# 59 tiles of 512 rows and 11 of 256 in the expert part, in place of 67 of 512

## The chip, the core and the metric

One core of a Trainium2 chip runs the whole kernel in one launch. The metric is the device time of that launch in microseconds. TensorE (PE), VectorE (DVE), ScalarE (ACT), GpSimd (POOL) and SyncE (SP) each run their own list of instructions in order and meet at semaphores. SP starts the loads; POOL starts the scattered stores. The order of all lists is written out by hand.

## What is computed

128 sequences of 124 tokens (15,872 tokens, 256 features) go through a tokenizer, one attention layer and a mixture of six experts of which each token uses two:

```
h = _L0_tok_ref(x, W, b, gamma, beta)
h = h + _L0_attn_ref(_layernorm(h), ...)          # 124 x 124 scores per sequence
# _L0_ffn_ref(f = _layernorm(h)), E = 6, TOP_K = 2:
rh = relu(f @ router_w1 + router_b1)
expert_logits = softmax(rh @ router_w2 + router_b2)
top_w, top_i = top_k(expert_logits, 2);  routing_weights = softmax(top_w)
h1 = relu(f @ expert_w1[e] + expert_b1[e])
h2 = relu(h1 @ expert_w2[e] + expert_b2[e])
expert_out = h2 @ expert_w3[e] + expert_b3[e]
h = h + sum over the two chosen experts of routing_weight * expert_out
```

So 31,744 pairs of token and expert go through three 256 x 256 layers. Every product is made three times, with high and low halves of both factors (hi*hi, hi*lo, lo*hi), to reach float32 accuracy on the fast path of TensorE.

## The kernel before

The **first part** (`pipeline(step)`) works through the sequences in 32 groups of four. Each token's normed features, its gates and its number are written by POOL (line 522) into `expert_rows`, a DRAM tensor with one region per expert, so that the rows of an expert stand together. `h` itself is stored to `out`.

The **second part** runs over `NT` = 67 tiles of `TILE` = 512 rows: the most that six experts can need when each one's last tile is filled up with pad rows. The first six tiles (`EARLY`) belong to the expert that leads after group 19 and start inside the first part. For the rest DVE makes a table on the chip (`tile_table_rows`, `tile_table_experts`: the row at which tile t starts, its expert, whether weights and biases change, and `ADD_AT`, the count of landed stores to wait for), SP writes it to DRAM and reads it back into `tab`.

Four steps make up one tile t:

- *turn* (line 782): TensorE transposes 4 x 2 blocks of `xg` into banks 0 and 1; ACT copies them to `xv` and makes `x_hi` (986, 989), DVE makes `x_lo` (1380).
- *first layer* (793), 12 products of 512 columns (2 output halves x 2 input halves x 3 variants) into banks 2 and 3; ACT makes `h1v` (996), DVE splits it into `h1_hi` and `h1_lo` (1395, 1380).
- *second layer* (793), 12 such products into banks 4 and 5; ACT makes `h2v` (1003), DVE splits it.
- *third layer* (820), 24 products of 256 columns into banks 6 and 7; DVE adds the bias into `yo` (1411), ACT multiplies by the gate (1009), POOL adds the 4 x 128 rows to `out` with four indirect stores that accumulate (570).

TensorE's order in step t is: first layer of t, turn of t+1, third layer of t-1, second layer of t. DVE's is: split h1 of t, low half of x of t+1 (`rows_low`), sums of t-1 (`rows_out`), split h2 of t. ACT's is: `h1v` of t, `xv` and `x_hi` of t+1, `h2v` of t, gates of t-1. Below, F, T, Th and S are short for first layer, turn, third layer and second layer.

POOL's `add_tile(t)` waits until the stores of tile t-2 have landed, because two experts' tiles may hold the same token. If tile t begins a new expert, it waits also for the stores of t-1 (`ADD_AT`). Tiles of one expert never share a token, so there the stores run on. `yo` has four buffers, `tail` (gates and token numbers) eight, `xg` and `small` four, `w_sb` two. SP loads 512 rows (530 KB) for each tile and 3 x 512 KB of weights only where the expert differs from that of two tiles before (`cond=`).

Of the kernel before, what the change touches and what calls it, by code (L numbers as in the profile page):

```python
# [11 lines left out]

# [16 lines left out]
P = 128  # L29
# [4 lines left out]
D = 256  # L34
# [14 lines left out]
TB = TILE // P  # L49
REGION = NTOK + TILE  # L50
NT = (NTOK * TOPK + NE * (TILE - 1)) // TILE
# [13 lines left out]
SPARE = NT - NTOK * TOPK // TILE  # L65
# [4 lines left out]
NORMS = 3  # L70
DRAIN = G + 1
assert (DECIDE + 1) * GT * TOPK > NE * (EARLY * TILE - 1)
# [16 lines left out]
def audio_tower(nc, x, tok_w, tok_b, tok_gamma, tok_beta, wq, bq, wk, bk, wv, bv, scale,  # L89
                rw1, rb1, rw2, rb2, eweights, esmall, out):  # L90
    with ExitStack() as ctx:  # L91
# [10 lines left out]
        tab_dram = nc.dram_tensor("tile_table", [NT, COLS], I32, kind="Internal").ap()  # L102

# [65 lines left out]
        tail = sb("tail", [P, TAILS, TB, REC - D])  # L169

# [6 lines left out]
        with ExitStack() as part_a:  # L177
# [37 lines left out]
            "tail_kept", "y_ps", "y_dve", "y_gated", "dve_passed", "pool_passed", "sp_passed")}  # L215
# [61 lines left out]
        def landed(t):  # L277

            return (t // 2 + 1) * ADDED if t >= 0 else 0

# [7 lines left out]
        def _(sp):  # L288
# [134 lines left out]
            def next_rows(t):  # L423
                if t < NT:
                    wait_apart(sp, S["txT_ps"], (t - SLOTS + 1) * 2, S["sp_passed"])
                    wait_apart(sp, S["tail_kept"], (t - SLOTS + 1) * 2, S["sp_passed"])
                    if t < EARLY:
                        early_rows(t)
                    else:
                        load_rows(t % SLOTS, table_of(t, ROW, NE * REGION + (SPARE - 1) * TILE))  # L430

# [7 lines left out]
            for t in range(SLOTS, EARLY):  # L439
                wait_apart(sp, S["y_dve"], (t - SLOTS + 1) * 4, S["sp_passed"])  # L440
# [10 lines left out]

            for t in range(1, NT):
                if EARLY <= t + WSLOTS < NT:
                    wait_apart(sp, S["h1_ps"], (t + 1) * 2, S["sp_passed"])
                    load_layers(t + WSLOTS, (0,))
                if t + SLOTS + 1 > EARLY:
                    next_rows(t + SLOTS + 1)
                if EARLY <= t + 1 < NT:
                    wait_apart(sp, S["y_ps"], t * 2, S["sp_passed"])
                    load_layers(t + 1, (2,))  # L460
                if EARLY <= t + SLOTS - 1 < NT:
                    wait_apart(sp, S["y_dve"], t * 4, S["sp_passed"])
                    load_small(t + SLOTS - 1)
                if EARLY <= t + WSLOTS < NT:
                    wait_apart(sp, S["h2_ps"], (t + 1) * 2, S["sp_passed"])
                    load_layers(t + WSLOTS, (1,))
            for i in range(2):
                sp.wait_ge(y_added[i], (NT - i + 1) // 2 * ADDED)

        @block.gpsimd  # L470
        def _(pool):
# [86 lines left out]
            def add_tile(t):  # L558

                wait(pool, y_added[t % 2], landed(t - 2))  # L560
                if t < EARLY:
                    wait(pool, y_added[(t - 1) % 2], landed(t - 3))
                else:
                    if t == EARLY:
# [904 lines left out]
```

## Time and profile before

| | us |
|---|---|
| median of three runs | 1250.46 (1249.2 to 1252.42) |
| the profiled execution | 1249.82 |
| span in its trace | 1248.0 |
| TensorE busy | 1197.6 (96%) |
| VectorE / ScalarE / GpSimd busy | 984.9 / 893.4 / 901.1 |

TensorE's granted clock was 0.989 of full speed over the span. The page says what each engine does in the whole; the stretch views cut the span into parts; the timeline gives single instructions with start, duration and, in brackets, the idle time before them and what ended it; the view of waits sums that idle time.

### The profile page before, as it was taken

What the parts mean: (1) busy time and instruction counts of PE and PEld (TensorE: products, weight loads), DVE (VectorE), ACT (ScalarE), POOL (GpSimd) and SP (SyncE); (2) the same over time, 40 slices, a digit from 0 to 9 for tenths busy, and PEclk for the clock granted to TensorE, in tenths of its full rate; (3) what the DMA queues carried; (4) which work ended last, traced back from release to release, by engine and by line L of the source; (5) the groups of instructions that cost most, each with busy time, mean ns of one, the idle gap of its engine ahead of it and who ended that gap; (6) DMA issues with size and microseconds to landing.
All of it is one profiled execution on the core that took longest, in us unless ns stands there. A gap on an engine that the chain in (4) does not pass through costs nothing. (4 is left out here: it accounts for less than half of the span.)

```text
span 1248.0 us, 27869 instructions
## 1 busy us (share of the span) xinstructions
PE 1197.6 (96%) x7792; PEld 1060.7 (85%) x7792; DVE 984.9 (79%) x3213; ACT 893.4 (72%) x2093; POOL 901.1 (72%) x684
## 2 busy tenths in 40 slices
PE   6999999999999999999789999999999999999993
PEld 5888988889888988887678888889888888888883
DVE  5678888888888988886796887778778777787773
ACT  4788888888888888887456667666676666766762
POOL 2227888888888888887788676767667667676776
PEclk9999999999999999999899999999999999999997
DMA  4334665554454545564589988776886797697655
GB/s 132 111 94 121 164 166 148 143 128 131 128 128 123 129 130 142 169 168 117 139 189 279 238 155 206 119 128 108 174 180 113 130 225 126 116 203 150 111 60 60
DMA packets 137190, 180.43 MB, mean 145 GB/s; under 512 B 38344, under 2 KB 103500, under 8 KB 137036
## 3 DMA queue, kind: packets, MB, share of 16 engines
q0 software_dynamic: 75456, 69.19, 34.5%
q1 hardware_dynamic: 60316, 108.67, 28.6%
q8 instruction: 63, 1.03, 0.3%
q10 hardware_dynamic: 1264, 0.79, 0.2%
q14 instruction: 91, 0.75, 0.2%
HBM read 159.01 MB, written 101.49 MB: 209 GB/s over the span
## 5 line engine op out<-in xcount | busy, mean ns | idle before, releaser
L570 POOL DMA_INDIRECT out<-yo,tail x268 | 432.5, 1614 | 169.1 <-issue 139.6
L522 POOL DMA_INDIRECT expert_rows<-rec,row_i x256 | 356.3, 1392 | 78.0 <-issue 67.2
L1003 ACT ACTIVATE h2v<-bank,small 128x512 f32<-128x512 f32 x134 | 92.3, 690 | 205.3 <-PE bank L793 189.8
L820 PE MATMUL bank<-w_sb,h_hi 128*128 128x256 f32 x1072 | 208.7, 288 | 3.5 <-issue 3.4
L793 PE MATMUL bank<-x_hi,w_sb 128*128 128x512 f32 x536 | 178.2, 394 | 6.1 <-DVE x_lo L1380 4.6
L793 PE MATMUL bank<-h_hi,w_sb 128*128 128x512 f32 x536 | 177.2, 391 | 1.8 <-issue 1.8
L820 PEld LDWEIGHTS bank<-w_sb,h_hi 128*128 128x128 f32 x1072 | 171.3, 191 | 4.4 <-issue 4.3
L820 PE MATMUL bank<-w_sb,h_lo 128*128 128x256 f32 x536 | 151.5, 283 | 0.0
L793 PEld LDWEIGHTS bank<-x_hi,w_sb 128*128 128x128 f32 x536 | 101.7, 190 | 27.9 <-issue 4.8
L793 PEld LDWEIGHTS bank<-h_hi,w_sb 128*128 128x128 f32 x536 | 100.9, 188 | 21.9 <-issue 1.9
L1009 ACT ACTIVATE yo<-yo,gcol 128x256 f32<-128x256 f32 x268 | 113.9, 498 | 4.5 <-DVE yo L1411 4.5
L1395 DVE CAST h_hi<-h1v 128x512 fp32r<-128x512 f32 x134 | 63.8, 476 | 64.1 <-ACT h1v L996 64.0
L584 PE MATMUL bank<-tok_proj,xT_hi 128*124 128x256 f32 x512 | 101.8, 292 | 9.0 <-DVE tok_proj L1029 9.0
L793 PE MATMUL bank<-x_lo,w_sb 128*128 128x512 f32 x268 | 105.2, 393 | 0.0
L793 PE MATMUL bank<-h_lo,w_sb 128*128 128x512 f32 x268 | 105.1, 392 | 0.0
L820 PEld LDWEIGHTS bank<-w_sb,h_lo 128*128 128x128 f32 x536 | 102.7, 192 | 0.0
L1395 DVE CAST h_hi<-h2v 128x512 fp32r<-128x512 f32 x134 | 59.0, 440 | 49.0 <-ACT h2v L1003 43.8
L1380 DVE TENSOR_TENSOR h_lo<-h1v,h_hi 128x512 fp32r<-128x512 f32 x134 | 93.0, 694 | 4.6
L1380 DVE TENSOR_TENSOR h_lo<-h2v,h_hi 128x512 fp32r<-128x512 f32 x134 | 92.9, 694 | 4.6
L584 PE MATMUL bank<-v_proj,xn1T_hi 128*124 128x256 f32 x512 | 94.7, 286 | 0.0
L513 POOL TENSOR_TENSOR rstd<-vareps,neghalf 124x8 f32<-124x8 f32 (+1 forms) x67 | 89.8, 1341 | 5.6
L1063 DVE BATCH_NORM_STATS2 stats<-h 124x6 f32<-124x256 f32 x256 | 89.4, 411 | 0.0
(193 smaller groups left out, 2975.9 us busy)
## 6 DMA issues: line engine op xcount, KB each, us to landing
w_sb<-split_weights SPq DMA_DIRECT2D x189, 512.0 KB
xg<-expert_rows SPq DMA_DIRECT2D x67, 530.0 KB
out<-h SPq DMA_DIRECT2D x32, 496.0 KB
split_weights<-half_w SPq DMA_DIRECT2D x36, 256.0 KB
small<-in_esmall SPq DMA_DIRECT2D x67, 134.0 KB
x_in<-in_x SPq DMA_DIRECT2D x32, 250.0 KB
expert_rows<-pad_rows SPq DMA_DIRECT2D x9, 530.0 KB
raw_w<-in_eweights SPq DMA_DIRECT2D x36, 128.0 KB
```

The source lines that it names most:

```text
L513: pool.tensor_tensor(rstd[0:TOK, norms, :], vareps[0:TOK, norms, :], neghalf[0:TOK, :].unsqueeze(1).to_broadcast([TOK, count, GB]), ALU.po ...
L522: pool.indirect_dma_start(rows_dram, bass.IndirectOffsetOnAxis(ap=row_i[0:TOK, slot, j, k:k + 1], axis=0), rec[0:TOK, slot, j, :], None).t ...
L570: pool.indirect_dma_start(out, bass.IndirectOffsetOnAxis(ap=tail[:, t % TAILS, j, E8:].bitcast(I32), axis=0), yo[:, t % YO, j, :], None, c ...
L584: mm = pe.matmul(bank, lhs[a], rhs[b], start=(first and n == 0), stop=(last and n == 2))
L793: mm = pe.matmul(banks[bank + m][:], w[:, n, c, wh, m * P:(m + 1) * P], act[:, c, :], start=(c == 0 and p == 0), stop=(c == DC - 1 and p = ...
L820: mm = pe.matmul(banks[6 + b][:, (j % 2) * D:(j % 2 + 1) * D], act[:, c, j * P:(j + 1) * P], w[:, 2, c, wh, :], start=(c == 0 and p == 0), ...
L1003: act.activation(h2v[:, m, :], banks[bank + m][:], ACT.Relu, bias=small[:, t % SLOTS, DC + m:DC + m + 1]).then_inc(S["h2_v"], 1)
L1009: act.activation(yo[:, t % YO, j, :], yo[:, t % YO, j, :], ACT.Identity, scale=gcol[:, t % YO, j:j + 1]).then_inc(S["y_gated"], 1)
L1063: v.bn_stats(stats[R, which, j, :], src(j)).then_inc(s, 1)
L1380: v.tensor_tensor(lo, val, hi.bitcast(F32), ALU.subtract).then_inc(ready, 1)
L1395: v.tensor_copy(hi[:, m, :], val[:, m, :]).then_inc(s, 1)
```

## The change

- `NT` becomes 59 tiles of 512 rows, the number that is full of real rows whatever the routing. What is left goes into `NH` = 11 tiles of `HALF` = 256 rows. Together 33,024 rows in place of 34,304.
- `ORDER` is the list of all 70 pieces. A half tile stands behind the big tiles 14, 18, ... 54. Each list of instructions now goes through `ORDER`, with the piece's place `q` in the counts of semaphores and 256 columns where 512 were.
- Half tiles have their own buffers: `half_xg` (one), `half_sb` for weights (one), `half_small` (one), `half_yo` and `half_tail` (two each). SP loads rows, biases and all three weights for each of them, without a condition (`half_rows`, `half_layers`, called from `half_loads` two and one big tiles ahead).
- DVE makes a second table behind piece 4 (`half_table`, 29 small instructions): row, expert, and the store counts `HOLD`, `HOLD_ODD`, `FOLLOW`. It takes a way through DRAM of its own.
- POOL's `add_half` waits for the stores of the big tile ahead of it if that has another expert (`HOLD`); the big tile behind it waits for the half tile's stores if it has another expert (`FOLLOW`).

```diff
-NT = (NTOK * TOPK + NE * (TILE - 1)) // TILE
+NT = (-(-NTOK * TOPK // HALF) - NE) // 2
+NH = (NTOK * TOPK + NE * (HALF - 1)) // HALF - 2 * NT
...
+FIRST_HALF, HALF_STEP = 14, 4
+HALF_RING = 2
...
+AFTER = [FIRST_HALF + HALF_STEP * k for k in range(NH)]
+ORDER = []
+for big in range(NT):
+    ORDER.append(Piece(len(ORDER), False, big, TB))
+    if big in AFTER:
+        ORDER.append(Piece(len(ORDER), True, AFTER.index(big), HB))
...
+            def half_layers(k, layers):
+
+                expert = half_table_of(k, HEXPERT, NE - 1)
+                for n in layers:
+                    if k:
+                        q = HALVES[k - 1].q
+                        wait_apart(sp, (S["h1_ps"], S["h2_ps"], S["y_ps"])[n], (q + 1) * 2, S["sp_passed"])
+                    sp.dma_start(half_sb[:, n, :, :, :].rearrange("p c b n -> p c (b n)").bitcast(F32),
+                                 split_dram[bass.ds(expert * (3 * DC) + n * DC, DC), :, :].rearrange("q p n -> p q n")
+                                 ).then_inc(half_w_loaded[n], 16)
+            def half_loads(t):
...
+                for k in range(NH):
+                    since = t - (FIRST_HALF + HALF_STEP * (k - 1))
+                    if since == 2:
+                        half_rows(k)
+                        half_layers(k, (0,))
+                    if since == 3:
+                        half_layers(k, (1, 2))
...
             def add_tile(t):
...
+                if t.n - 1 == AFTER[0] or t.n - 2 in AFTER:
+                    pool.wait_ge(S["half_added"], sum(a < t.n for a in AFTER) * HALF_ADDED)
+                elif t.n - 1 in AFTER:
+                    at = half_value(AFTER.index(t.n - 1), FOLLOW)
+                    wait_apart(pool, S["half_added"], at, S["pool_passed"])
+                add_rows(t, y_added[t.n % 2])
+            def add_half(t):
+
+                if t.n == 0:
+                    pool.wait_ge(S["half_tab_loaded"], 16)
+                even, odd = half_value(t.n, HOLD), half_value(t.n, HOLD_ODD)
+                wait_apart(pool, y_added[0], even, S["pool_passed"])
+                wait_apart(pool, y_added[1], odd, S["pool_passed"])
+                add_rows(t, S["half_added"])
...
             def layer(t, n, bank, hi, lo, read, count, done):
-                w = w_sb[t % WSLOTS]
+                w, cols = weights_in(t), t.blocks * P
...
-                            mm = pe.matmul(banks[bank + m][:], w[:, n, c, wh, m * P:(m + 1) * P], act[:, c, :],
+                            mm = pe.matmul(banks[bank + m][:, 0:cols], w[:, n, c, wh, m * P:(m + 1) * P], act[:, c, 0:cols],
                                            start=(c == 0 and p == 0), stop=(c == DC - 1 and p == 2))
```

What stands in a row on TensorE. Before, between the first layer of a tile (lines with `x_hi`, `x_lo`) and its second, there is a turn and a whole third layer (24 products, of which the first stand here):

```order
L793 MATMUL bank<-x_hi,w_sb 128x512
L782 MATMUL bank<-ident,xg 128x128 x8
L820 MATMUL bank<-w_sb,h_hi 128x256
L820 MATMUL bank<-w_sb,h_lo 128x256
L820 MATMUL bank<-w_sb,h_hi 128x256 x2
L820 MATMUL bank<-w_sb,h_lo 128x256
L820 MATMUL bank<-w_sb,h_hi 128x256 x2
L820 MATMUL bank<-w_sb,h_lo 128x256
```

In the changed kernel, at the big tile behind a half tile (`half_sb` holds the half tile's weights):

```order
L961 MATMUL bank<-x_hi,w_sb 128x512
L950 MATMUL bank<-ident,xg 128x128 x8
L989 MATMUL bank<-half_sb,h_hi 128x256
L989 MATMUL bank<-half_sb,h_lo 128x256
L989 MATMUL bank<-half_sb,h_hi 128x256 x2
L989 MATMUL bank<-half_sb,h_lo 128x256
L989 MATMUL bank<-half_sb,h_hi 128x256 x2
L989 MATMUL bank<-half_sb,h_lo 128x256
L989 MATMUL bank<-half_sb,h_hi 128x256 x2
L989 MATMUL bank<-half_sb,h_lo 128x256
L989 MATMUL bank<-half_sb,h_hi 128x256
L961 MATMUL bank<-h_hi,w_sb 128x512
```

The third layer between the two is now 12 products, so the second layer of that big tile stands 12 products nearer to its first.

On POOL, the stores of two tiles in a row before, with the semaphores that each waits for:

```order
L566 TENSOR_LOAD tab [waits y_added0]
L566 ISA x2
L570 DMA out<-yo,tail 16896x256 [waits y_added1,y_gated]
L570 DMA out<-yo,tail 16896x256 x3
L566 TENSOR_LOAD tab [waits y_added1]
L566 ISA x2
L570 DMA out<-yo,tail 16896x256 [waits y_added0,y_gated]
```

And in the changed kernel from a half tile to the big tile behind it:

```order
L735 DMA out<-half_yo,half_tail 16896x256 [waits y_added0,y_added1,y_gated]
L735 DMA out<-half_yo,half_tail 16896x256
L710 TENSOR_LOAD tab [waits y_added1]
L710 ISA x2
L720 TENSOR_LOAD half_tab [waits y_added0]
L720 ISA x2
L735 DMA out<-yo,tail 16896x256 [waits half_added,y_gated]
L735 DMA out<-yo,tail 16896x256 x3
```

Two stores more stand between the tiles' stores, with a wait for both counts of big stores ahead of them and a wait for `half_added` behind them.

On DVE, behind the last split of piece 4's h2, the split of piece 5's h1 came next before:

```order
L1380 TENSOR_TENSOR h_lo<-h2v,h_hi 128x512 [waits h2_split]
L1395 CAST h_hi<-h1v 128x512 [waits h1_v]
L1380 TENSOR_TENSOR h_lo<-h1v,h_hi 128x512 [waits h1_split]
L1395 CAST h_hi<-h1v 128x512 [waits h1_v]
L1380 TENSOR_TENSOR h_lo<-h1v,h_hi 128x512 [waits h1_split]
```

Now the second table stands between them; its first and its last rows are

```order
L1616 TENSOR_TENSOR h_lo<-h2v,h_hi 128x512 [waits h2_split]
L1554 TENSOR_TENSOR u_pairs<-t_nt,t_cum 124x8
L1555 TENSOR_SCALAR u_halves<-t_i 124x8
L1556 TENSOR_SCALAR u_at<-t_iota 124x1
L1558 TENSOR_SCALAR u_next<-t_iota 124x1 x2
L1562 TENSOR_SCALAR u_pairs<-u_pairs 124x8 [waits halves,near]
...
L1610 TENSOR_SCALAR u_cols<-u_cols 124x1 [waits halves]
L1613 CAST u_coli<-u_cols 124x5 [waits halves]
L1633 CAST h_hi<-h1v 128x512 [waits h1_v]
```

The split of piece 5's h1 moved behind 29 small instructions.

## Rows read from the trace of the kernel before

**Rows 1.** Page, part 1: busy us, share of the span, instructions.
```profile
PE 1197.6 (96%) x7792; PEld 1060.7 (85%) x7792; DVE 984.9 (79%) x3213; ACT 893.4 (72%) x2093; POOL 901.1 (72%) x684
```

**Rows 2.** Stretches: length, then busy (count) of PE, PEld, DVE, ACT, POOL; clock, DMA.
```profile
510.00:700.00 190.00, 175.00 (x1106) 151.34 (x1105) 150.40 (x535) 124.27 (x283) 148.52 (x113) 0.98 0.71 181
700.00:1200.00 500.00, 499.90 (x3034) 444.87 (x3033) 396.97 (x867) 332.55 (x652) 356.72 (x221) 1.00 0.77 150
```

**Rows 3.** View of waits, TensorE, 720 to 1240 us: total, times, longest.
```profile
PE bank L820 <- issue: 2.0, 1, 2.0
```

**Rows 4.** Timeline of TensorE over one tile: start, us, instruction.
```profile
901.01 0.40 PE L793 MATMUL bank<-h_hi,w_sb 128*128 128x512 f32 x1
...
903.76 0.39 PE L793 MATMUL bank<-x_hi,w_sb 128*128 128x512 f32 x1
...
906.49 1.03 PE L782 MATMUL bank<-ident,xg 128*128 128x128 f32 x8
907.28 0.36 PE L820 MATMUL bank<-w_sb,h_hi 128*128 128x256 f32 x1
...
907.60 0.40 PE L820 MATMUL bank<-w_sb,h_hi 128*128 128x256 f32 x2
...
907.96 0.40 PE L820 MATMUL bank<-w_sb,h_hi 128*128 128x256 f32 x2
...
910.24 0.40 PE L793 MATMUL bank<-h_hi,w_sb 128*128 128x512 f32 x1
```

**Rows 5.** Timeline of ScalarE and of VectorE over the same tile.
```profile
904.55 1.70 ACT L1009 ACTIVATE yo<-yo,gcol 128x256 f32<-128x256 f32 x4
906.15 1.25 ACT L996 ACTIVATE h1v<-bank,small 128x512 f32<-128x512 f32 x2
...
906.85 0.43 DVE L1395 CAST h_hi<-h1v 128x512 fp32r<-128x512 f32 x1 [1.01 <-ACT h1v L996]
...
908.47 0.69 DVE L1380 TENSOR_TENSOR h_lo<-h1v,h_hi 128x512 fp32r<-128x512 f32 x1
```

**Rows 6.** Timeline near the end: last h2 split, and the third layer behind it.
```profile
1226.85 0.69 DVE L1380 TENSOR_TENSOR h_lo<-h2v,h_hi 128x512 fp32r<-128x512 f32 x1
...
1227.64 0.36 PE L820 MATMUL bank<-w_sb,h_hi 128*128 128x256 f32 x1 [2.01 <-issue]
```

**Rows 7.** Timeline of POOL: stores at new experts (tiles 15, 44, 64) and at 59.
```profile
772.23 1.56 POOL L570 DMA_INDIRECT out<-yo,tail  x1 [5.28 <-issue]
...
1033.24 1.68 POOL L570 DMA_INDIRECT out<-yo,tail  x1 [0.30 <-issue]
1037.97 1.54 POOL L570 DMA_INDIRECT out<-yo,tail  x1 [3.05 <-DMA out<-yo,tail]
...
1174.32 1.66 POOL L570 DMA_INDIRECT out<-yo,tail  x1 [1.83 <-issue]
...
1221.44 1.69 POOL L570 DMA_INDIRECT out<-yo,tail  x1 [2.88 <-DMA out<-yo,tail]
```

**Rows 8.** Stretches as in rows 2, around loads of weights, last two: DMA share, GB/s.
```profile
735.00:767.00 32.00, 32.00 (x190) 28.25 (x189) 26.25 (x57) 20.38 (x40) 25.06 (x16) 1.00 1.01 233
...
1034.00:1038.00 4.00, 4.00 (x30) 3.68 (x29) 2.88 (x6) 4.00 (x10) 0.95 (x2) 1.00 0.58 76
...
660.00:665.00 5.00, 3.55 (x17) 2.58 (x15) 2.52 (x5) 2.97 (x6) 4.39 (x3) 1.00 1.13 317
```

**Rows 9.** Timelines of VectorE (table, first and last) and TensorE around piece 5.
```profile
643.16 0.15 DVE L1362 TENSOR_TENSOR t_cols<-t_row,t_first 124x1 f32<-124x1 f32 x1
...
644.35 0.17 DVE L1377 CAST t_coli<-t_cols 124x5 int32<-124x5 f32 x1
...
655.10 1.09 PE L782 MATMUL bank<-ident,xg 128*128 128x128 f32 x8 [2.27 <-DMA xg<-expert_rows]
...
663.27 0.50 PE L793 MATMUL bank<-x_hi,w_sb 128*128 128x512 f32 x1 [1.45 <-DMA w_sb<-split_weights]
```

**Rows 10.** Page, part 6: issues of weight loads and their size.
```profile
w_sb<-split_weights SPq DMA_DIRECT2D x189, 512.0 KB
```

More of the change, by code:

```diff
@@ L13 @@
+from collections import namedtuple
 from contextlib import ExitStack
@@ L70 @@
 NORMS = 3
+HROW, HEXPERT, HOLD, HOLD_ODD, FOLLOW, HCOLS = range(6)
+HALVES_AT = 27
+FIRST_HALF, HALF_STEP = 14, 4
+HALF_RING = 2
 DRAIN = G + 1
+Piece = namedtuple("Piece", "q half n blocks")
+AFTER = [FIRST_HALF + HALF_STEP * k for k in range(NH)]
+assert AFTER[-1] + 2 < NT and FIRST_HALF % 2 == 0 and HALF_STEP % 2 == 0
+ORDER = []
[3 more added lines that the diff above has]
+        ORDER.append(Piece(len(ORDER), True, AFTER.index(big), HB))
+BIG = [t for t in ORDER if not t.half]
+HALVES = [t for t in ORDER if t.half]
 assert (DECIDE + 1) * GT * TOPK > NE * (EARLY * TILE - 1)
@@ L279, in landed, with gated_up_to, rows_in, kept_tail @@
             return (t // 2 + 1) * ADDED if t >= 0 else 0
+        def gated_up_to(q):
+            return sum(t.blocks for t in ORDER[:max(q, 0)])
+        def rows_in(t):
+            return half_xg[:] if t.half else xg[:, t.n % SLOTS, :, :]
+        def kept_tail(t):
+            return half_tail[:, t.n % HALF_RING, :, :] if t.half else tail[:, t.n % TAILS, :, :]
+        def small_in(t):
+            return half_small[:] if t.half else small[:, t.n % SLOTS, :]
+        def sums_out(t):
+            return half_yo[:, t.n % HALF_RING, :, :] if t.half else yo[:, t.n % YO, :, :]
+        def gate_out(t):
+            return half_gcol[:] if t.half else gcol[:, t.n % YO, :]
+        def weights_in(t):
+            return half_sb if t.half else w_sb[t.n % WSLOTS]
+        def rows_here(eng, t):
+            if t.half:
+                eng.wait_ge(S["half_rows_loaded"], 16 * (t.n + 1))
+            else:
+                eng.wait_ge(rows_loaded[t.n % SLOTS], t.n // SLOTS * 16 + 16)
+        def small_here(eng, t):
+            if t.half:
+                eng.wait_ge(S["half_small_loaded"], 16 * (t.n + 1))
+            else:
+                eng.wait_ge(small_loaded[t.n % SLOTS], t.n // SLOTS * 16 + 16)
+        def layer_here(eng, t, n):
+            if t.half:
+                eng.wait_ge(half_w_loaded[n], 16 * (t.n + 1))
+            else:
+                eng.wait_ge(w_loaded[t.n % WSLOTS][n], fetched(t.n))
+        def added_before(eng, t, ring):
+            if t.half:
+                wait(eng, S["half_added"], (t.n + 1 - HALF_RING) * HALF_ADDED)
+            else:
+                wait(eng, y_added[t.n % 2], landed(t.n - ring))
         def sent_to(slot, groups):
@@ L577, in _ @@
+            for t in ORDER:
+                if t.half:
+                    add_half(t)
+                else:
+                    add_tile(t)
         @block.tensor
@@ L1399, in rows_out @@
             def rows_out(t):
-                at = t * 4
-                wait(v, S["y_gated"], (t - 1) * TB)
-                wait(v, y_added[t % 2], landed(t - YO))
-                v.wait_ge(small_loaded[t % SLOTS], t // SLOTS * 16 + 16)
-                v.tensor_tensor(gsel[:], tail[:, t % TAILS, :, 0:E8],
-                                small[:, t % SLOTS, 2 * DC + D:SMALL].unsqueeze(1).to_broadcast([P, TB, E8]),
+                at, each = t.q * 4, t.blocks // 2
+                gates_of = half_gsel[:] if t.half else gsel[:]
```

362 lines of the change are left out of this document (242 added, 120 removed).

## The prediction

> **What bounds the kernel now.** I read the page first: TensorE is busy 96% of the span, no other engine above 79% [rows 1]. Since such shares are a mean over stages, the stretch view comes next. From 510 to 700 us, where both parts overlap, TensorE idles 15 of 190 us; from 700 to 1200 us it is busy for 499.9 of 500 us at a granted clock of 1.00, while VectorE, ScalarE and GpSimd have 21%, 33% and 29% to spare [rows 2]. The view of waits agrees: from 720 to 1240 us TensorE waits once, for 2.0 us, at the last tile [rows 3]. So the second part lasts as long as TensorE's own work, until something else comes late. The timeline gives that work for a tile of 512 rows: S takes 2.75 us (901.01 to 903.76), F 2.73 (to 906.49), T 0.79 (to 907.28), Th 2.96 (to 910.24); one tile is 9.23 us from S to S [rows 4]. The product of 512 columns costs 2.73 / 12 = 0.2275 us, that of 256 columns (907.60 to 907.96 for three) 0.12 us [rows 4].
>
> **TensorE's work.** The change takes 8 tiles of 512 away (67 to 59) and puts 11 of 256 in. A half tile costs on TensorE: F 12 x 0.12 = 1.44; T 4 of 8 transposes, 0.40; Th 12 of 24 products, 12 x 0.12 plus the 0.08 by which the first product behind a turn is longer (2.96 - 24 x 0.12), 1.52; S 1.44. Sum 4.80 us, which is 0.18 more than half a tile. So -8 x 9.23 + 11 x 4.80 = -73.8 + 52.8 = **-21.0 us**, all on the path, since nothing else ends a wait there. The 0.12 is from the third layer, whose products have the same shape (128 x 128 weights, 256 columns) as the half tile's first two. If a half product cost just half of one of 512 columns (0.114), 24 of them would bring 0.15 us per half tile, 1.6 in all: -22.6.
>
> The Trainium skill (TensorE: Matmul & The Clock Gate, "Wait — 56ns, not 53.3ns?") puts matmuls in a row at columns / 2.4 GHz plus about 2.5 ns. For 256 columns that is 109 ns. The trace's 120 ns stands against it [rows 4], and by the page's figure the 36 products of a half tile would be 0.4 us cheaper and the sum about 4 us lower.
>
> **Which step gets tight.** Let F of a half tile start at 0, with the big tile p ahead of it and n behind. TensorE: F(half) to 1.44, T(n) to 2.23, Th(p) to 5.19, S(half) to 6.63, F(n) to 9.37, T to 10.16, Th(half) to 11.68, S(n). Two waits shrink. (a) Th(p) needs the split of h2(p), which is done 2.08 us after S ends when it runs at the usual pace; the same split at the end of the kernel lets Th start 0.10 us behind its own end [rows 6]: 2.18 against 2.23, no stall, no reserve. (b) S(n) needs the split of h1(n). In the trace this ends at 908.47 + 0.69 = 909.16, or 2.67 behind the end of F [rows 5]; with 0.10 to start, 2.77. Before, T and Th (3.75) covered it. Behind a half tile they last 0.79 + 1.52 = 2.31, so S(n) would stall 0.46. But the chain starts with ScalarE, which comes to h1v only after four gates (904.55 to 906.15 [rows 5]), 0.34 before F ends. In the step of the half tile its own evictions are short (I take 0.42 for 256 columns against the 0.69 of 512), so gates of p are done at about 8.8 and h1v(n) begins 0.57 before F(n) ends; the second half of h1v still waits for the end of F. That leaves a stall of about 0.1. Bounds 0 to 0.46 each; I take 0.1: 11 x 0.1 = **+1.1** (0 to 5.1).
>
> **The second table** is 29 instructions on VectorE behind piece 4. Nine of the first table took 643.16 to 644.52, or 0.15 us each [rows 9], so 29 are some 4.4 to 5 us. They are ahead of the split of h1(5), hence of S(5). But TensorE waits there anyway: 2.27 us for the rows of tile 6 at 655.10, then 1.45 for its weights at 663.27 [rows 9], and neither comes by way of the new table. Th(4) and S(5) follow the turn: S(5) would start at 655.10 + 0.79 + 2.96 = 658.85. The split of h1(5), now done near 659.2, holds it 0.4 us, and the second wait swallows this. Value **0**; if the cover goes, 5.
>
> **The end.** Before, the stores of the first spare tile (64) waited 2.88 us for another expert's to land [rows 7], started 1.0 us later than one tile period behind the last, and the two tiles after it ran back to back. The changed kernel has no big spare tile, and its last change of expert is at tile 54 of 59. POOL's list ends the kernel in both, about **-1.1**.
>
> **Moved, at no cost.** SP issues five more transfers per half tile; they stand at the end of an iteration, behind them the next tile's loads, which have 15 us or more before use. The accumulating stores fall from 268 to 258. ScalarE and VectorE do less. For each half tile 3 x 512 KB of weights are loaded [rows 10], with rows and biases 1.9 MB, 21 MB in all, while 8 row loads go (4 MB). Their cover is lead time: rows and first layer are issued at the end of S two big tiles ahead of the half tile's own, 9.23 + 2.73 = 12.0 us before the turn, layer two at the end of S one ahead, 9.23 + 5.19 = 14.4 us before S(half); the existing loads have 2 x 9.23 - 2.73 = 15.7 us. In 735 to 767 us, where an expert changes and 3 MB of weights come in at 233 GB/s, TensorE ran 32.00 of 32.00 us [rows 8]. So I take 0.
>
> Sum against the profiled execution: -21.0 + 1.1 + 0 - 1.1 = -21.0, so 1249.8 - 21.0 = 1228.8; the median of runs lies 0.6 higher, so **1229.5 us**.
>
> **Rivals.** *The split is late and the table is bare* (0.46 x 11 + 4.8 = 9.9 instead of 1.1): 1238. For it: the exact numbers of rows 5; (a) has no reserve, and if h2's split slips by 0.3 it costs 3.3 by itself. Against: ScalarE's shorter step.
>
> *POOL becomes the bound by its waits for landing.* By the routing of these inputs the experts take 1507, 2940, 8278, 9131, 5406 and 4482 rows; nine half tiles are real, one of expert 2 and eight of expert 5, and they stand among tiles of experts 1 to 4. Ten of eleven therefore wait for the big tile before, and make the one behind wait. At the steady pace the gap before a tile's four stores is 1.83 [rows 7], so they take 9.23 - 1.83 = 7.4 us, and the gap can shrink to the 0.30 that stands between stores. A cycle is four big tiles (29.6), three such gaps (0.9), a half tile (two stores, 3.4) and two waits L: 33.9 + 2L, against 4 x 9.23 + 4.80 + 0.1 = 41.8 of TensorE. L below 3.9 costs nothing. L was 3.05 and 2.88 at tiles 44 and 64, but 5.28 at tile 15, amid a load of weights [rows 7]. With 5.28 in all of nine cycles POOL is 24 us behind at tile 50 and makes up 12 by the end: 1241. For it: the new loads start in each cycle near the second wait. Against: that row is one of six changes of expert.
>
> *The half tile's weights or rows come late* — the one that ends on the other side. Each wait costs all of itself, 11w: w = 1.9 eats the gain, from 2.25 the kernel is slower by over 0.3%. At 660 to 665 us with 317 GB/s TensorE was busy only 3.55 of 5 us [rows 8], and it lost 2.27 and 1.45 us to transfers [rows 9]; with w = 3.7, their sum, the time is 1229.5 + 41 = 1270. Against: 32 of 32 us busy at 233 GB/s [rows 8], and of 11 half tiles only those at 14, 30, 42 and 54 have a change of expert beside them. At w near 1.9 the change brings nothing, which is my case for no difference.
>
> The Trainium skill (DMA: Bandwidth & Descriptors, "Issuing engines are not separate DMA queues") says that transfers from SP, ACT and POOL run on the same 16 DMA engines and interleave. It speaks for both of these rivals: loads lengthen the landing of stores. The trace agrees in one place, tile 15.
>
> *Half products at half the price* (0.114 or less): 1226 to 1228.
>
> **Chances.** Forecast, with 1227.5 to 1233: 0.58. Late split and bare table, to 1239: 0.19. POOL: 0.09. Cheaper products: 0.03. Late loads, slower: 0.06; late loads near 1.9 us each, no difference: 0.05. About 0.3% (3.75 us) is what a measurement of this kernel can tell from none. Faster 0.89, same 0.05, slower 0.06. The range 1226 to 1240 holds the first, most of the second, the fourth and a part of POOL's.
>
> **What would show it.** From 760 us to the end of TensorE's work it should be busy in all but 1 to 2 us, with 59 and 11 tiles. Right: second layers of n behind a DVE split by about 0.1 us; products on `half_sb` 0.12 us apart; POOL's gaps at half tiles about 3 us. Wrong: waits of TensorE for `half_sb` or `half_xg`; VectorE waiting for `half_added` or `y_added`; POOL without any gap other than landings from tile 18 on; a wait at S(5) that moves all that follows.

## The result, and the profile after

| | before | changed |
|---|---|---|
| median of runs | 1250.34 us (8 runs) | 1243.05 us (8 runs, 1241.32 to 1245.25) |
| ratio to before | | 0.9948, 95% interval 0.9936 to 0.9959 |
| profiled execution, its span | 1249.8, 1248.0 us | 1241.32, 1239.5 us |

The change gains 7.3 us where 21 were forecast. It is faster, but the time lies above the range of 1226 to 1240.

I compare along the *turns*, the starts of the eight (or four) transposes of a piece's rows on TensorE, because they show where in the kernel a microsecond goes. In the traces:

| | before | changed | forecast for changed |
|---|---|---|---|
| turn of the piece behind big tile 14 | 740.6 | 741.8 | 740.6 |
| turn of the last big tile | 1210.6 | 1202.3 | 1190.7 |
| from there to the end of the span | 37.4 | 37.2 | 36.3 |

So 1.1 us are lost ahead of the first half tile, 10.5 between it and the last turn (460.5 us where 450.1 were forecast), and 0.9 at the end: 12.5, which is all that separates 1241.3 from 1228.8.

The page (as [rows 1]) and the stretches (as [rows 2]) of the changed kernel:

```profile
PE 1182.3 (95%) x7784; PEld 1050.0 (85%) x7784; DVE 982.0 (79%) x3290; ACT 887.6 (72%) x2107; POOL 885.7 (71%) x674
...
700.00:1200.00 500.00, 493.06 (x3085) 442.02 (x3084) 399.10 (x933) 332.29 (x676) 351.01 (x216) 1.00 0.84 184
```

TensorE idles 6.9 us in the 500 in which it idled 0.1 before. The view of waits, TensorE from 720 to 1240 us, names them (as [rows 3]; total, times, longest):

```profile
PE bank L961 <- DMA half_sb<-split_weights: 6.6, 4, 2.7
PE bank L989 <- issue: 2.0, 1, 2.0
PE bank L961 <- issue: 0.2, 1, 0.2
```

It is the weights of half tiles. TensorE's timeline has the four places, each the second layer of a half tile:

```profile
755.93 0.39 PE L961 MATMUL bank<-h_hi,half_sb 128*128 128x256 f32 x1 [2.73 <-DMA half_sb<-split_weights]
...
925.79 0.39 PE L961 MATMUL bank<-h_hi,half_sb 128*128 128x256 f32 x1 [0.61 <-DMA half_sb<-split_weights]
...
1053.00 0.39 PE L961 MATMUL bank<-h_hi,half_sb 128*128 128x256 f32 x1 [1.42 <-DMA half_sb<-split_weights]
...
1180.78 0.38 PE L961 MATMUL bank<-h_hi,half_sb 128*128 128x256 f32 x1 [1.83 <-DMA half_sb<-split_weights]
```

These are the half tiles behind big tiles 14, 30, 42 and 54, just the four with a change of expert beside them. Behind the first wait the granted clock falls. The stretches from 755 us show it (the column behind the engines' counts):

```profile
755.00:760.00 5.00, 4.07 (x17) 3.73 (x18) 1.90 (x5) 1.86 (x5) 3.08 (x2) 0.66 1.11 334
760.00:770.00 10.00, 10.00 (x58) 8.59 (x57) 7.65 (x18) 7.06 (x14) 6.45 (x4) 1.00 1.02 253
```

An undisturbed cycle of four big tiles and a half tile lasts 41.84 us from turn to turn; this one lasts 46.2, that is 4.4 more, of which 2.73 are the wait and most of the other 1.7 goes to products at 1.2 instead of 2.4 GHz. So this wait costs more than the view of waits says.

A half tile where nothing is late, on TensorE's timeline (turn of the half tile, third layer of the tile before, second layer of it, first layer of the half tile, next turn):

```profile
830.12 0.60 PE L950 MATMUL bank<-ident,half_xg 128*128 128x128 f32 x4
830.48 0.36 PE L989 MATMUL bank<-w_sb,h_hi 128*128 128x256 f32 x1
...
833.42 0.40 PE L961 MATMUL bank<-h_hi,w_sb 128*128 128x512 f32 x1
...
836.17 0.28 PE L961 MATMUL bank<-x_hi,half_sb 128*128 128x256 f32 x1
836.28 0.28 PE L961 MATMUL bank<-x_lo,half_sb 128*128 128x256 f32 x1
...
837.60 1.04 PE L950 MATMUL bank<-ident,xg 128*128 128x128 f32 x8
```

Twelve products of the first layer take 837.60 - 836.17 = 1.43 us, 0.12 each. One step later, where the next big tile's second layer waits for the split of its h1:

```profile
847.18 0.69 DVE L1616 TENSOR_TENSOR h_lo<-h1v,h_hi 128x512 fp32r<-128x512 f32 x1
...
847.98 0.47 PE L961 MATMUL bank<-h_hi,w_sb 128*128 128x512 f32 x1
```

The split ends at 847.87 and the layer starts 0.11 behind it.

### The profile page after: what moved, and what is told of

It reads as the page before. It is cut to its first block, busy times and chain, and to the rows that moved or that the text cites. A ratio compares the mean times of both kernels' runs of the same rounds, so it can differ in the third digit from the quotient of the medians.

```text
span 1239.5 us, 28038 instructions
## 1 busy us (share of the span) xinstructions
PE 1182.3 (95%) x7784; PEld 1050.0 (85%) x7784; DVE 982.0 (79%) x3290; ACT 887.6 (72%) x2107; POOL 885.7 (71%) x674
## 4 chain that ended last, share of the span: by engine, by line
PE 53%; ACT 11%; SPq 10%; issue 9%; DVE 7%; POOL 5%; DMA 4%; POOLq 0%; ACTq 0%; DVEq 0%
PE bank L961 17%; PE bank L752 12%; PE bank L989 8%; SPq L496 6%; POOL expert_rows L666 3%; PE bank L906 3%; PE bank L807 3%; PE bank L950 2%; PE bank L892 2%; ACT rec L1056 2%; DMA half_sb<-split_weights 2%; ACT square L1097 2%; DVE h L1372 2%; SPq L503 2%; PE bank L798 2%
## 5 line engine op out<-in xcount | busy, mean ns | idle before, releaser
L735 POOL DMA_INDIRECT out<-yo,tail x236 | 384.0, 1627 | 128.5 <-issue 71.2
L989 PE MATMUL bank<-w_sb,h_hi 128*128 128x256 f32 x944 | 184.9, 289 | 3.6 <-issue 3.6
L961 PE MATMUL bank<-x_hi,w_sb 128*128 128x512 f32 x472 | 157.8, 395 | 5.5 <-DVE x_lo L1616 4.6
L961 PE MATMUL bank<-h_hi,w_sb 128*128 128x512 f32 x472 | 157.2, 394 | 3.8 <-issue 2.3
L989 PEld LDWEIGHTS bank<-w_sb,h_hi 128*128 128x128 f32 x944 | 151.7, 192 | 4.3 <-issue 4.2
L1633 DVE CAST h_hi<-h1v 128x512 fp32r<-128x512 f32 (+1 forms) x140 | 60.8, 434 | 56.7 <-ACT h1v L1167 56.7
L1633 DVE CAST h_hi<-h2v 128x512 fp32r<-128x512 f32 (+1 forms) x140 | 58.8, 420 | 47.9 <-ACT h2v L1175 46.1
L1616 DVE TENSOR_TENSOR h_lo<-h2v,h_hi 128x512 fp32r<-128x512 f32 (+1 forms) x140 | 91.6, 654 | 4.8
L1616 DVE TENSOR_TENSOR h_lo<-h1v,h_hi 128x512 fp32r<-128x512 f32 (+1 forms) x140 | 91.5, 653 | 4.8
L1616 DVE TENSOR_TENSOR x_lo<-xv,x_hi 128x512 fp32r<-128x512 f32 (+1 forms) x140 | 85.0, 648 | 6.0 <-ACT x_hi L1159 6.0
```

Source lines behind the costliest of these rows:

```text
L735: pool.indirect_dma_start(out, bass.IndirectOffsetOnAxis(ap=kept_tail(t)[:, j, E8:].bitcast(I32), axis=0), sums_out(t)[:, j, :], None, com ...
L961: mm = pe.matmul(banks[bank + m][:, 0:cols], w[:, n, c, wh, m * P:(m + 1) * P], act[:, c, 0:cols], start=(c == 0 and p == 0), stop=(c == D ...
L989: mm = pe.matmul(banks[6 + b][:, i * D:(i + 1) * D], act[:, c, j * P:(j + 1) * P], w[:, 2, c, wh, :], start=(c == 0 and p == 0), stop=(c = ...
L1616: v.tensor_tensor(lo, val, hi.bitcast(F32), ALU.subtract).then_inc(ready, 1)
L1633: v.tensor_copy(hi[:, m, 0:cols], val[:, m, 0:cols]).then_inc(s, 1)
```

## Experiments

Two theories on the late weights came first. **S**: SyncE's list of instructions has no time left, so that transfers at its end are issued late. **D**: they are issued in time and the DMA engines, busy with the loads of a new expert, bring them late. S begins with two rows. The first is SyncE's timeline around half tile 42, whose turn is at 1040.20: the prediction had layers two and three issued 2.7 us ahead of that turn, and they are issued 6.25 behind it.

```profile
1035.74 0.38 SPq L535 DMA_DIRECT2D half_sb<-split_weights  x1
...
1046.45 1.04 SPq L535 DMA_DIRECT2D half_sb<-split_weights  x2
```

Layer one, forecast 12.0 us ahead of the turn, goes out 4.5 ahead of it (1035.74). But for its wait of 1.42 us, TensorE would have begun the second layer at 1051.58, 5.1 us behind the issue of its weights; and the view of `half_sb` puts issue to landing at 5.3 us in the median, 3.6 to 8.1. The second is what SyncE does all the time. Before each transfer it reads the tile's row, expert or a flag from the table, and such a read (`value_load`, line 496 of the changed kernel, 403 of before) is three instructions:

```profile
L496 SPq TENSOR_LOAD <-tab x407: 260/270/841, 720.0 to 1199.8; - x136
L496 SPq FUSED_REGOPS  x406: 147/152/164, 720.3 to 1198.2; - x136
L496 SPq SEQ_ASSERT  x406: 18/18/18, 720.5 to 1198.5; - x136
```

270 + 152 + 18 ns is 0.44 us, and a big tile has nine of them, 4.0 us of 9.22, beside five transfers (0.34 to 0.38 us each where they move something) and their waits. From 720 to 1200 us SyncE waits for other engines for 32.0 us altogether; in the kernel before it was 29.3. The sum is no smaller, but it isn't there where it is needed: ahead of the late layers SyncE waits 0.0 us (740 to 756), 1.7 (908 to 926), 1.3 (1036 to 1054) and 0.0 (1164 to 1181), ahead of one in time 3.3 (992 to 1010).

### Fewer reads and more reads

`e2_held` keeps each value in a register once it is read, so that a big tile has four reads instead of nine, and a half tile two instead of four:

```
 def table_of(t, column, most):
-    return sp.value_load(tab[0:1, bass.ds(t * COLS + column, 1)], ...)
+    if (t, column) not in held:
+        ...
+        held[t, column] = sp.value_load(tab[0:1, bass.ds(t * COLS + column, 1)], ...)
+    return held[t, column]
```

> The changed kernel, with one thing other: SyncE reads each number of the two tables once and keeps it in a register, 4 reads per big tile instead of 9 and 2 per half tile instead of 4. A read is about 0.45 us of SyncE's list (0.27 + 0.15 + 0.02), so its list gets some 2.2 us shorter per big tile. Same transfers, same bytes, same order. Theory S (SyncE's list is full, so that the half tiles' weights are issued 5 to 8 us late): layer two of a half tile is issued some 6 us sooner against the turn of the half tile (before: 3.8 to 8.4 us behind its start), TensorE's waits for half_sb (6.6 us in 4) and the fall of the clock behind the first (1.7) go, time 1243 - 8 = 1235, between 1233 and 1237. Theory D (the 16 DMA engines are too busy, transfers land late): the waits stay, 1243 within 2.

Measured: **1254.12 us** (1244.72 to 1257.72, ten runs), ratio 1.0026 (1.0005 to 1.0047). By its time this refutes both. By its trace it bears S out, and shows something behind it. SyncE now waits 193.4 us from 720 to 1200, and layers two and three of half tile 42 go out at 1037.26, 0.4 ahead of its turn at 1037.7. TensorE, from 720 to 1240 us, waits for nothing but the last tile:

```profile
PE bank L999 <- issue: 2.0, 1, 2.0
PE bank L971 <- issue: 0.8, 3, 0.3
```

Its last turn is at 1196.0, 6.3 us earlier than in the changed kernel. But the span goes on for another 56.2 us instead of 37.2, since GpSimd is still storing. Its timeline at half tile 38 (two stores) and at the end:

```profile
1040.37 1.78 POOL L745 DMA_INDIRECT out<-half_yo,half_tail  x1 [6.06 <-DMA out<-yo,tail]
...
1049.02 1.54 POOL L745 DMA_INDIRECT out<-yo,tail  x1 [5.03 <-issue]
...
1245.98 1.54 POOL L745 DMA_INDIRECT out<-yo,tail  x1 [0.30 <-issue]
```

From tile 14 to tile 58 every gap on GpSimd but those for landing is 0.3 us, the pace at which it never waits for work. Theory **P** starts here: with SyncE mended, GpSimd is the bound, by its waits for landing.

`e3_more` and `b3_more` go the other way: one more read in each call of `load_layers`, three a tile, in the changed kernel and in the kernel before.

```
         fresh = table_of(t, NEW_W, 1)
+        table_of(t, NEW_SMALL, 1)
```

> The changed kernel with one table read more in each call of load_layers, whose value is not used: three per big tile, about 1.4 us of SyncE's list, no transfer more. Theory S: an iteration of SyncE goes from some 8.4 us to 9.8 and four of them with a half tile from about 40 to 45, against TensorE's 41.8, so SyncE becomes the bound: over 11 such cycles 30 to 40 us more, 1270 to 1285. Theory D: 1243 within 2.

Measured: **1303.6 us** (one run).

> The kernel before with the same extra table reads. Theory S: an iteration of 9.8 us against TensorE's 9.22 falls behind by 0.6 us per tile. The loads have 15.7 us of lead at the time they are due, which hides a part; about 60 tiles, so 36 us behind at the end less some 10 of lead: 1265 to 1280. Theory D: 1250 within 2.

Measured: **1311.32 us** (one run). Both are slower than S expected, and D, which expected nothing, is out: reading a table alone costs 61 us over 63 tiles, 1.0 of the 3 x 0.44 = 1.3 us a tile. So the kernel before had some 0.3 to 0.4 us a tile to spare, although its TensorE waited for nothing. SyncE itself now waits for no other engine at all: from 720 to 1200 us its view of waits is empty in `b3_more`, where the kernel before has 29.3 us. Waits of TensorE from 720 to 1240 us, `e3_more` first, then `b3_more`:

```profile
PE bank L962 <- DMA half_sb<-split_weights: 29.1, 10, 5.7
PE bank L951 <- DMA half_xg<-expert_rows: 14.0, 4, 10.2
PE bank L990 <- DMA w_sb<-split_weights: 1.4, 2, 0.8
```

```profile
PE bank L794 <- DMA w_sb<-split_weights: 31.3, 24, 3.9
PE bank L821 <- DMA w_sb<-split_weights: 4.3, 6, 1.3
```

`b2_held` is the control, the held values in the kernel before.

> The kernel before with each table value kept in a register. In its second part TensorE waits for nothing and there are no half tiles. Both theories: 1249 to 1251 us, no change, since SyncE's list was just short enough. If the start of the second part (2.3 and 1.5 us of waits at 655 and 663 us) hangs on SyncE's list too, 1246 to 1248 us.

Measured: **1250.87 us**, ratio 1.0004 (0.9995 to 1.0014). SyncE now waits 191.9 us of the 480 where it waited 29.3, and the time stays: its list costs nothing until it is full.

### Half tiles' weights issued elsewhere

`e1_early` issues the three layers together, one big tile earlier for layers two and three:

```
             half_rows(k)
-            half_layers(k, (0,))
-        if since == 3:
-            half_layers(k, (1, 2))
+            half_layers(k, (0, 1, 2))
```

> The changed kernel, with layers two and three of a half tile's weights issued behind layer one, an iteration of SyncE sooner. Same transfers, two table reads of a half tile fewer. Theory S: they land 9 us sooner, no wait for half_sb, 1235 (1233 to 1238). Theory D: 1.9 MB now come in one burst; landing gets longer (median 5.3 us before), rows and layer one of the half tile or the next tile's loads come late in their place, 1240 to 1245.

Measured: median **1240.81 us**, ratio 0.9919 (0.9903 to 0.9936); four runs lie at 1239.6 to 1241.0 and two at 1256.7 and 1257.4, and the profiled one is of the two. In its trace no wait for `half_sb` is left, the last turn is at 1200.9, and GpSimd, without reserve from tile 14 on, ends 53.8 us behind it. In the profiled run there are new waits of 1.2 us for the half tile's rows at 743 and of 4.2 us for `w_sb` at 1175. The median lies in D's range and not in S's, but D is out by the extra reads, and a full list explains the new waits as well: what now stands behind the six transfers goes out late (rival F below). The kernel makes one read less for each half tile, not two as expected.

`e9_apart` issues layers one and two some 22 us ahead of the half tile's turn (at the turn 1043.78) and layer three 13 us ahead, where in the changed kernel layer one goes out 2 to 5 us ahead and the others 4 to 8 us behind; rows and biases stay where they were, and so do the first half tile's weights. `e8_held_apart` is the same with held values.

```
     load_layers(t + WSLOTS, (0,))
+if t - 1 in AFTER[:-1]:
+    half_layers(AFTER.index(t - 1) + 1, (0, 1))
 ...
+if t - 1 in AFTER[:-1]:
+    half_layers(AFTER.index(t - 1) + 1, (2,))
 half_loads(t)
```

> The changed kernel with only the issue of the half tiles' weights moved, as in the run before this, and every table value read anew. Theory S (SyncE's list is full, and the transfers for half tiles 14, 30, 42 and 54 come late since they stand at its end): a lead of a whole tile more takes the 6.6 us of waits for half_sb away, 1235 to 1238 us, if the tile's own weights and rows do not become late in their place. Rival F (the list stays full and something behind it in the list becomes late instead): waits for w_sb or xg of 5 us and more, 1241 to 1248 us.

Measured: **1243.06 us**, ratio 0.9944 (0.9927 to 0.9961): rival F. The wait for weights has moved down the same list, to the half tiles' rows. Waits of TensorE from 640 to 1240 us (the one for `xg` is the wait at 656 us that the kernel before has too; the one for `half_sb` is at the first half tile):

```profile
PE bank L955 <- DMA half_xg<-expert_rows: 5.7, 6, 1.3
PE bank L955 <- DMA xg<-expert_rows: 3.1, 1, 3.1
PE bank L966 <- DMA half_sb<-split_weights: 2.4, 1, 2.4
```

> SyncE keeps each table value in a register as in the run with held values, and from the second half tile on the three weight transfers of a half tile are issued one big tile after the half tile before: layers one and two at the start of that tile's part of SyncE's list (about 15 us behind that half tile's turn), layer three at its end (22 us), rows and biases where they were. Theory P (with held values TensorE was served but GpSimd became the bound, since its two waits for landing in a cycle, some 25 to 28 and 31 to 35 us behind the turn, had moved into the weight transfers, and being late put them deeper in): the transfers now lie ahead of both waits, the gaps shrink from 3.2 to 6.6 us to about 3.2, GpSimd keeps pace, and the time is 1234 to 1238 us. Rival Q (GpSimd is late for another reason, such as its own count of stores or the gates): it stays at 1250 to 1256 us with waits for landing of 5 us and more. Rival R (the second state of TensorE's waits comes back, since SyncE's list is in another order): waits for half_sb or w_sb of some us and 1240 to 1245 us.

Measured: **1241.35 us**, ratio 0.9937 (0.9915 to 0.9958), and last turn at 1193.7. The time is in R's range, but none of R's waits is there: TensorE waits for no weights behind 663 us. It is 12.8 us faster than `e2_held` and 3.4 slower than P's upper bound: GpSimd's gaps at half tiles and behind them shrank only from 4.9 to 4.3 us in the mean of 18, where 3.2 was expected, and it still has no reserve.

`e10_held_no_w` loads the weights of the first half tile alone and leaves out the loads for the other ten, which are multiplied by the first one's weights.

```
 def half_layers(k, layers):
+    if k:
+        return
```

> Held table values, and the weights of the half tiles are loaded for the first one alone: the other ten multiply by the first one's weights, so this part of the result is left out. 15.7 MB of transfers go and nothing else. Theory P (weight transfers lengthen the landing that GpSimd waits for): gaps of about 3.1 us at each half tile and behind it, GpSimd keeps pace, 1233 to 1237 us. Rival Q (landing or lateness do not come from the weight transfers): 1248 to 1256 us as with held values alone. For TensorE alone both expect the last turn at 1195 to 1197 us in the trace, as with held values.

Measured: **1239.38 us** (two runs), last turn at 1194.0. Again in P's direction (14.7 us below `e2_held`) and again short of its numbers: the mean gap is 4.2 us, with single ones of 5.5 and 7.3. So weight loads make up only part of what a store's landing takes; what the rest is, these runs leave open.

### Half the waits for landing

The pace of GpSimd is told best by the two kernels in which it never waited for work between half tiles 18 and 50, eight cycles: they take 355 us in `e2_held` (44.4 each) and 341.7 in `e10_held_no_w` (42.7). Less the two gaps of 4.9 and of 4.2 this leaves 34.6 and 34.3 us of its own work. TensorE's cycle is 41.9, so a gap may be 3.7 us; more than that is lost, in every cycle. If P is right, fewer waits must help even when each stays as long as it is. The next three kernels store half tiles in pairs: the sums of one wait in `half_yo` (two slots) until the next is ready.

```
 for t in ORDER:
     if not t.half:
         add_tile(t)
     elif t.n % 2 == 0:
         hold(t)
         if t.n:
             add_rows(HALVES[t.n - 1], S["half_added"])
         add_rows(t, S["half_added"])
```

The waits on `half_added` follow (only behind even half tiles, and VectorE's for a whole pair). It relies on both half tiles of a pair having one expert, as they have with these inputs.

> The run with held table values and the half tiles' weights one tile earlier, and in addition GpSimd stores the half tiles in pairs: the sums of half tiles 2 and 3 (counted from 1) both go behind big tile 22, those of 4 and 5 behind tile 30 and so on, so that a pair needs one wait for landing ahead of it and one behind it; eleven half tiles then take 11 to 12 such waits where they took 20. The number of stores stays. Theory P (with SyncE mended GpSimd is the bound, and by its waits for landing): five cycles lose some 9 us each, GpSimd keeps pace with TensorE, the last turn stays at 1193 to 1195 us and the kernel ends 37 us behind it: 1231 to 1234 us. Rival Q (GpSimd is bound by its own 258 stores, which no wait hides): no change, 1240 to 1242 us. Rival L (two half tiles' stores in a row make the landing longer by what the second wait saved): 1237 to 1241 us.

Measured: **1233.9 us**, ratio 0.9877 (0.9860 to 0.9893), last turn at 1194.2, end 38.2 us behind it.

> Held table values and paired stores, the half tiles' weights issued where the changed kernel has them. With held values alone the time was 1254.1 us and TensorE's last turn at 1196.0. Theory P: half the waits for landing are gone, even at 5 to 6.5 us each GpSimd needs 67.5 + 2 x 6 = 80 us for eight big tiles and two half tiles against 83.8 of TensorE, so 1232 to 1237 us. Rival Q: 1250 to 1256 us.

Measured: **1232.59 us**, ratio 0.9875 (0.9859 to 0.9892), last turn at 1192.9, end 37.9 us behind it. Against `e2_held` it differs in the pairs alone, and is 21.5 us faster by the medians (18.9 by the two ratios to the kernel before). Both kernels lie in P's range. A pair on GpSimd's timeline:

```profile
1020.44 1.54 POOL L750 DMA_INDIRECT out<-half_yo,half_tail  x1 [3.22 <-DMA out<-yo,tail]
1022.29 1.54 POOL L750 DMA_INDIRECT out<-half_yo,half_tail  x1 [0.30 <-issue]
1024.13 1.73 POOL L750 DMA_INDIRECT out<-half_yo,half_tail  x1 [0.30 <-issue]
1026.17 1.76 POOL L750 DMA_INDIRECT out<-half_yo,half_tail  x1 [0.30 <-issue]
1033.96 1.54 POOL L750 DMA_INDIRECT out<-yo,tail  x1 [6.03 <-ACT yo L1201]
```

The second wait is as long as ever (6.03; the releaser named had gated these rows long before, so it is the landing). But there is one for two half tiles, and at tiles 44 and 45 gaps of 1.1 and 1.5 us are back, the mark of a GpSimd that waits for work (1.8 us in the steady pace of [rows 7]). TensorE from 700 to 1200 us in the same trace:

```profile
700.00:1200.00 500.00, 499.20 (x3138) 448.35 (x3137) 406.15 (x947) 338.32 (x688) 357.45 (x218) 1.00 0.84 182
```

> The changed kernel with the paired stores alone; SyncE's list as it is. Theory S (in the changed kernel itself the late weights are what ends last, GpSimd only follows): within 2 us of the changed kernel, 1241 to 1244 us, with the waits of TensorE for half_sb as before and GpSimd idle 10 us and more in a cycle. Rival P2 (GpSimd holds the changed kernel already): 1234 to 1239 us.

Measured: **1240.43 us** (1237.23 to 1242.66), ratio 0.9934 (0.9913 to 0.9956). TensorE still waits 3.8 us for `half_sb`, the end is 37.7 us behind the last turn. That is between both expectations, and the interval overlaps that of the changed kernel: GpSimd cost the changed kernel itself 0 to some 5 us, not more. Read against `e13_held_pairs`, which differs from it in the held values alone and is 7.8 us faster, this run gives the price of SyncE's full list in a kernel where GpSimd has a reserve.

> Paired stores as in the run at 1240.4 us, every table value read anew as in the changed kernel, and layers two and three of a half tile's weights issued together with layer one, one big tile earlier. Theory S (the place of these transfers in SyncE's full list is what cost the changed kernel its gain, and GpSimd only gave it back where it was the bound): the waits for half_sb (3.8 us in the run with pairs alone, 6.6 in the changed kernel) go, the last turn comes at 1193 to 1197 us as with held values, 1232 to 1237 us. Rival F (the six transfers in a row only move the lateness to the tile's own weights and rows, since the list is as long as before): waits for w_sb, xg or half_xg of 4 us and more, 1238 to 1242 us.

Measured: **1241.55 us**, ratio 0.9913 (0.9896 to 0.9930): rival F. No wait for `half_sb`, but the list is as long as before but for one read, and what stands behind the six transfers is late instead:

```profile
656.86 1.97 PE L958 MATMUL bank<-ident,xg 128*128 128x128 f32 x8 [4.36 <-DMA xg<-expert_rows]
...
743.64 0.66 PE L958 MATMUL bank<-ident,half_xg 128*128 128x128 f32 x4 [2.11 <-DMA half_xg<-expert_rows]
...
1178.25 0.58 PE L997 MATMUL bank<-w_sb,h_hi 128*128 128x256 f32 x1 [5.28 <-DMA w_sb<-split_weights]
```

All runs in one table:

| kernel | us | last turn | from it to the end of the span |
|---|---|---|---|
| before | 1250.3 | 1210.6 | 37.4 |
| before, held values | 1250.9 | 1213.1 | 37.4 |
| before, three reads more a tile | 1311.3 | 1272.1 | 37.4 |
| changed | 1243.1 | 1202.3 | 37.2 |
| changed, three reads more a tile | 1303.6 | 1264.5 | 37.2 |
| early | 1240.8 (profiled run 1256.7) | 1200.9 | 53.8 |
| apart | 1243.1 | 1205.8 | 37.2 |
| pairs | 1240.4 | 1199.3 | 37.7 |
| early, pairs | 1241.6 | 1204.3 | 37.2 |
| held | 1254.1 | 1196.0 | 56.2 |
| held, apart | 1241.4 | 1193.7 | 45.2 |
| held, ten half tiles' weights left out | 1239.4 | 1194.0 | 43.0 |
| held, apart, pairs | 1233.9 | 1194.2 | 38.2 |
| held, pairs | 1232.6 | 1192.9 | 37.9 |

Whoever reads the last two columns sees both causes. SyncE's list decides the third column: among the kernels with half tiles, 1192.9 to 1196.0 with held values, 1199.3 to 1205.8 without, 1264.5 with more reads. GpSimd decides the fourth: 37 to 38 where it has a reserve, up to 56 where it has none. Only a kernel with both mended has the gain. `e13_held_pairs` beats both kernels, the one before by 1.2%.

Why is landing longer where SyncE is faster? In the changed kernel GpSimd's waits at half tile 38 fall into a quiet stretch, in `e2_held` into the loads for the next one (last two numbers: DMA share and GB/s; gap 3.26 and 6.06):

```profile
1023.00:1028.00 5.00, 5.00 (x34) 4.59 (x33) 3.93 (x11) 2.36 (x5) 1.74 (x2) 1.00 0.26 37
```

```profile
1036.00:1041.00 5.00, 5.00 (x38) 4.63 (x37) 3.89 (x11) 3.73 (x10) 0.63 (x1) 1.00 1.07 330
```

The same holds over all 36 such gaps of the two kernels (18 each, tiles 18 to 51). Where the stretch of the gap has under 60 GB/s, in 13 of them, the gap is 3.1 to 3.7 us; where it has over 160, in 14, it is 4.4 to 6.6 us, but for one of 3.2. The changed kernel has 11 of the first kind and 3 of the second, `e2_held` 2 and 11.

A GpSimd that is late comes to wait amid these loads, and each such wait makes it later. This would also give `e1_early` its two levels, 16 us apart. Both fit the rows, but no run fixed the moment of the loads alone, so it is argued, not shown.

## Why the prediction was wrong

**TensorE's work, -21.0: right.** The quiet cycle is 41.84 us where 4 x 9.23 + 4.80 + 0.1 = 41.8 were forecast; the product of 256 columns is 0.12 us, as forecast. The estimate of 109 ns from the rule of the Trainium skill (TensorE: Matmul & The Clock Gate, "Wait — 56ns, not 53.3ns?") is too low for these products. With 9.22 a big tile a half tile comes to 4.96 to 4.98 with its stall, 0.9 us in eleven more than forecast. The changed kernel's last turn is 8.3 us ahead of that of before; with SyncE and GpSimd mended it is 17.7 ahead, of 19.9 forecast.

**The stall at S(n), +1.1: right in size.** S(n) starts 0.11 behind the split and 0.13 behind the third layer (847.98 above), 0.1 us a half tile. The view of waits has 0.2 us for it, once.

**The second table, 0: right.** It takes VectorE 3.96 us, less than the 4.4 to 5 that were forecast:

```profile
653.49 0.16 DVE L1554 TENSOR_TENSOR u_pairs<-t_nt,t_cum 124x8 f32<-124x8 f32 x1
...
657.28 0.17 DVE L1613 CAST u_coli<-u_cols 124x5 int32<-124x5 f32 x1
...
658.94 0.69 DVE L1616 TENSOR_TENSOR h_lo<-h1v,h_hi 128x512 fp32r<-128x512 f32 x1
```

The split of h1(5) ends at 659.63, 0.2 behind the third layer of tile 4, and TensorE then waits for weights at 663.60 as before. The 1.1 us lost ahead of the first half tile come from a second wait for `w_sb`, at 671.49 [1.13]. Only the kernels with more reads have it too, and `e12_pairs`, whose SyncE has the same list, has not, so what brings it stays open.

**The end, -1.1: wrong, -0.2.** The stores of the third tile from the end do start 1.0 us earlier against the last turn, as forecast (1212.04 against 1202.28; before, 1221.44 against 1210.64). But the tile behind it then waits 1.1 us for its gates, where before it ran on, and only 0.5 us reach the last store:

```profile
1220.38 1.54 POOL L735 DMA_INDIRECT out<-yo,tail  x1 [1.09 <-ACT yo L1181]
...
1233.30 1.54 POOL L735 DMA_INDIRECT out<-yo,tail  x1 [0.30 <-issue]
```

**"SP issues five more transfers per half tile": the step that failed.** The prediction counted transfers and what lies behind them, and never the reads of the table ahead of them, nor how full SyncE's list was. Four reads (1.8 us) and five transfers of 0.34 to 0.38 us, with their waits, are about as much as the 4.98 us that a half tile adds on TensorE, and the list ahead had 0.3 to 0.4 us a tile to spare. At a change of expert, where six weight transfers of the big tiles move data (0.37 us each, against 0.08 where the condition says no), there is next to nothing left. Hence the "14.4 us before S(half)" were 3.0, 5.9, 5.1 and 4.4 us at half tiles 14, 30, 42 and 54 (from the issue to where S(half) would have begun without its wait) and 5.7 to 7.5 at the other seven; with held values they are 11.4 to 12.6. It cost 6.6 us of waits and 2.3 beyond them, most of that the lower clock behind the first (the excess of the three disturbed cycles, 4.4 + 0.9 + 1.8, less their waits): with the 0.9 above this makes up the 10.5 us but for 0.7.

The Trainium skill (DMA: Bandwidth & Descriptors, "Issuing engines are not separate DMA queues") says that starting transfers from several engines saves only the sequencer's time, "which is usually small relative to the DMA itself". For a single transfer the trace agrees: 0.38 us to issue, 5.3 to land. But the transfers overlap and the issues, with the reads ahead of each, don't, and so the list is the bound here.

The rival *the half tile's weights or rows come late* had the four places right by name, and named the wrong cause, bandwidth. It asked for a wait at each of eleven half tiles and set the change of expert against itself as rare; four waits, with a mean w of 1.65, were enough to take 8.9 of the 21 us.

The rival *POOL becomes the bound* had the mechanism right. Its 33.9 us of own work were 34.4, its bound for L so 3.7 instead of 3.9, and L was 4.9 us in the mean once SyncE was mended. It got 0.09, and only one L of the trace of before was above 3.9. In the changed kernel the mean of 18 gaps is 3.7, just at the bound:

```profile
1026.48 1.54 POOL L735 DMA_INDIRECT out<-half_yo,half_tail  x1 [3.26 <-DMA out<-yo,tail]
...
1033.82 1.92 POOL L735 DMA_INDIRECT out<-yo,tail  x1 [3.96 <-issue]
```

The range ended where the kernels with one of the two causes mended begin. It left out that a cause which is no resource in any view, the time of a sequencer that is never counted as busy, could take some 40% of the gain.

## What to carry to other kernels

An engine that only issues transfers shows no busy time. Add up its list over one period (reads into registers, transfers, waits) or take its waits in a quiet stretch as the reserve, before giving it anything more. When such a list is full, moving a transfer within it only moves the wait; shortening the list helps. And a step whose price is a wait for landing should be made rarer rather than faster: two half tiles behind one wait brought 19 to 21.5 us once SyncE's list was in order.

## What the runs showed of the hardware

- A read of a table value in SBUF into a SyncE register costs 0.44 us in a row (270 + 152 + 18 ns), more than issuing a transfer of 512 KB (0.37 us); nine of them a tile were 43% of SyncE's time.
- The landing of an accumulating store of 128 rows, from the end of its issue to the next store that waits for it, took 3.1 to 3.7 us in stretches under 60 GB/s and, but for one of 3.2, 4.4 to 6.6 us in stretches of 160 to 332 GB/s (36 gaps of the changed kernel and of `e2_held`).
- One idle time of 2.73 us on TensorE was followed by a granted clock of 0.66 over five microseconds, 1.2 GHz for about two thirds of them. Idle times of 0.6 to 1.8 us were followed by a clock of 1.00 and cost 0.3 us beyond their own length. The length of the idle time alone does not tell which it will be: in `b3_more` one of 3.67 us (at 757.48) was followed by 0.50 over five microseconds, one of 3.15 (at 1055.06) by 1.00.
